# A graph and feed-forward kernel: one of nine one-hot columns moves from VectorE to ScalarE in the last adding stage

## The reference, cut to what matters

```
time_feat = relu(edge_attr @ W_time.T + b_time)          # (212500, 64)
sums      = segment_sum(time_feat, src, n)               # (12500, 64)
counts    = segment_sum(ones, src, n)
node_time = sums / max(counts, 1)
fused     = relu([relu(ln(x) @ W_down.T + b_down), node_time] @ W_fusion.T + b_fusion)
x = x + ln(x) + fused @ W_up.T + b_up
x = x + shared_mlp(ln(x)) + top2_of_4_experts(ln(x))
```

## Time and profile before

| | us |
|---|---|
| median of 3 runs | 2168.73 |
| lowest and highest | 2162.14, 2173.69 |
| profiled execution | 2177.41 |
| its span | 2175.5 |

### The profile page before, as it was taken

The page is one execution under the profiler, slowest core; times in us unless marked ns, Lnnn a source line. Parts: engine busy times, 40 slices in busy tenths (PEclk is TensorE's granted clock), DMA queues, the critical chain, the costliest instruction groups (busy, mean ns, idle before and its releaser), DMA issues.

```text
span 2175.5 us, 75498 instructions
## 1 busy us (share of the span) xinstructions
PE 2000.5 (92%) x26922; PEld 1672.3 (77%) x26946; DVE 1779.5 (82%) x5883; ACT 1404.0 (65%) x3239; POOL 1069.4 (49%) x918
## 2 busy tenths in 40 slices
PE   4788888999999999999999999677869999999998
PEld 1576776799988899999899999677756667666666
DVE  9788999899988999998788887688966767767675
ACT  2598898999989888888988887000014444444443
POOL 0577777778787777787777776100011111111110
PEclk7699999999999999999999999899989999999999
DMA  2244343677766677776778776676731111212110
GB/s 85 71 127 122 126 126 122 189 213 208 211 198 180 205 219 220 217 217 200 208 226 245 239 223 183 178 205 184 205 96 44 53 58 44 66 44 66 44 54 31
DMA packets 239411, 323.68 MB, mean 149 GB/s; under 512 B 42144, under 2 KB 213965, under 8 KB 238706
## 3 DMA queue, kind: packets, MB, share of 16 engines
q1 hardware_dynamic: 176564, 192.90, 32.6%
q0 software_dynamic: 41504, 103.41, 13.0%
q10 hardware_dynamic: 20970, 22.54, 3.7%
HBM read 186.34 MB, written 175.77 MB: 166 GB/s over the span
## 4 chain that ended last, share of the span: by engine, by line
PE 71%; DVE 11%; DMA 5%; ACT 5%; issue 4%; SPq 1%; DVEq 1%; ACTq 1%; POOL 1%; POOLq 0%
PE moved L686 16%; PE bank L715 15%; PE bank L803 10%; PE bank L672 7%; PE moved L816 7%; PE bank L690 4%; DMA arena<-table 3%; DVE arena L1133 2%; PE bank L843 2%; DMA table<-arena 2%; DVE arena L1134 2%; PE bank L699 2%; ACT arena L1590 1%; DVE arena L1334 1%; ACT arena L1596 1%
## 5 line engine op out<-in xcount | busy, mean ns | idle before, releaser
L1812 POOL DMA_INDIRECT table<-arena x832 | 970.3, 1166 | 377.2 <-issue 262.3
L1596 ACT ACTIVATE arena<-moved 128x588 bf16<-128x588 f32 x832 | 547.0, 662 | 108.2 <-PE moved L686 91.7
L686 PE MATMUL moved<-arena 128*128 128x196 bf16 x4992 | 590.5, 254 | 7.8 <-ACT arena L1596 6.7
L686 PEld LDWEIGHTS moved<-arena 128*128 128x128 f16 x4992 | 453.6, 98 | 79.8 <-ACT arena L1596 19.1
L1590 ACT ACTIVATE arena<-bank 128x512 f32<-128x512 f32 x624 | 371.0, 595 | 84.0 <-PE bank L672 68.0
L1235 DVE TENSOR_TENSOR sums<-sums,bank 128x130 f32 x816 | 232.0, 284 | 109.4 <-PE bank L715 88.9
L715 PE MATMUL bank<-arena 128*128 128x64 bf16 (+1 forms) x7344 | 273.4, 194 | 37.2 <-DVE sums L1235 24.6
L715 PE MATMUL bank<-arena,w_all 128*128 128x64 bf16 (+1 forms) x7344 | 272.4, 194 | 19.4 <-DVE sums L1235 18.9
L1711 ACT ACTIVATE arena<-bank,w_all 128x512 f32<-128x512 f32 (+1 forms) x225 | 152.8, 679 | 207.8 <-PE bank L803 116.6
L715 PEld LDWEIGHTS bank<-arena 128*128 128x128 bf16 x7344 | 254.7, 98 | 41.7 <-DVE arena L1215 41.7
L715 PEld LDWEIGHTS bank<-arena,w_all 128*128 128x128 bf16 x7344 | 254.2, 98 | 23.8 <-DVE w_all L1215 23.7
(11 more groups left out here) (292 smaller groups left out, 2864.8 us busy)
## 6 DMA issues: line engine op xcount, KB each, us to landing
arena<-table SPq DMA_DIRECT2D x672, 147.0 KB
arena<-in_attr SPq DMA_DIRECT2D x208, 144.0 KB
arena<-table ACTq DMA_DIRECT2D x144, 147.0 KB
table<-arena POOLq DMA_INDIRECT x832
x_ln<-arena SPq DMA_DIRECT2D x98, 128.0 KB
arena<-in_x SPq DMA_DIRECT2D x97, 128.0 KB
arena<-x_ln SPq DMA_DIRECT2D x24, 512.0 KB, 4.6
out_rows<-arena SPq DMA_DIRECT2D x24, 512.0 KB, 3.2
```

The source lines that it names most:

```text
L686: mm = e.matmul(moved8[:, 4 * (n % 2) + h, 0:PW], slot_hot[s % NSLOT][:, t, h * P:(h + 1) * P], upper(s, 0, PW)[:, t, :], start=j == 0, st ...
L1596: e.activation(row_buf[n % NROWS], moved8[:, 4 * (n % 2):4 * (n % 2) + 3, 0:PW], ACT.Copy).then_inc(s_rows, 1)
L1812: e.indirect_dma_start(out=table, out_offset=bass.IndirectOffsetOnAxis(ap=dest[s % NDEST][:, a:a + 1], axis=0), in_=row_buf[n % NROWS].rea ...
```

## The change

For loads 2 to 95 of the last part, VectorE's comparison of the third third covers two columns and not three. The ninth column is made by ScalarE: Square of (number - iota), with the column of numbers as bias, into a scratch `apart`, then Relu of (1 - that), which is one where the two are equal and zero elsewhere. `apart` lies in the first scatter buffer. In ScalarE's program the passes for load n+1 stand behind its DMA issues of iteration n. TensorE waits for the new semaphore `s_hot_last` before the third third of such a load.

```diff
+        apart = row_buf[0].rearrange("p h w -> p (h w)")[:, 0:NODES_A_BUCKET]
...
+        def last_by_scalar(k, n, c):
+            return k == LAST and n >= 2 and c == CL - 1
...
             def add_up(k, n, c):
                 t = sum_first[k] + n
                 e.wait_ge(s_hot, CL * t + c + 1)
+                if last_by_scalar(k, n, c):
+                    e.wait_ge(s_hot_last, n - 1)
...
             def hot_piece(k, n, c):
                 t = sum_first[k] + n
-                lo_of = tab[t % NTB].rearrange("p c r (h w) -> p (c r h) w", h=BLOCK)[:, c * PIECE:(c + 1) * PIECE, LO:LO + 2]
-                e.tensor_tensor(in_pairs(hot[t % 2][:, c * PIECE:(c + 1) * PIECE]), pairs(iota_lo, PIECE), each_pair(lo_of, NODES_A_BUCKET), ALU.is_equal).then_inc(s_hot, 1)
+                columns = slice(c * PIECE, (c + 1) * PIECE - last_by_scalar(k, n, c))
+                lo_of = tab[t % NTB].rearrange("p c r (h w) -> p (c r h) w", h=BLOCK)[:, columns, LO:LO + 2]
+                e.tensor_tensor(in_pairs(hot[t % 2][:, columns]), pairs(iota_lo, columns.stop - columns.start), each_pair(lo_of, NODES_A_BUCKET), ALU.is_equal).then_inc(s_hot, 1)
...
+            def last_column(n):
+                t = sum_first[LAST] + n
+                e.wait_ge(s_table[t % NTB], 16 * CL * (t // NTB + 1))
+                at = (CL * BLOCK - 1) * PW + LO
+                lo_of = tab[t % NTB].rearrange("p c r w -> p (c r w)")[:, at:at + 1]
+                if n > 2:
+                    e.wait_ge(s_hot_last, n - 2)
+                e.activation(apart, iota_lo, ACT.Square, bias=lo_of, scale=-1.0).then_inc(s_apart, 1)
+                e.wait_ge(s_apart, n - 1)
+                e.wait_ge(s_sum_ps, CL * (t - 1))
+                e.activation(hot[t % 2][:, TC - 1], apart, ACT.Relu, bias=1.0, scale=-1.0).then_inc(s_hot_last, 1)
+
             for k, n in last_turns:
                 for m in turn_loads(k, n):
                     if m % 2:
                         load_chunks(e, row_reg, k, m, m == 1)
+                if 2 <= n + 1 < loads[k]:
+                    last_column(n + 1)
```

More of the change, by code:

```diff
@@ L121, in gnn_ffn @@
         s_unused = sem("s_unused")
-        s_hot, s_sum_ps, s_added = sem("s_hot"), sem("s_sum_ps"), sem("s_added")
+        s_hot, s_apart, s_hot_last, s_sum_ps, s_added = sem("s_hot"), sem("s_apart"), sem("s_hot_last"), sem("s_sum_ps"), sem("s_added")
         s_mean_a, s_square_a, s_sd_a, s_rs_a = sem("s_mean_a"), sem("s_square_a"), sem("s_sd_a"), sem("s_rs_a")
```

## The result

| | before | after |
|---|---|---|
| median us (12 runs each) | 2169.45 | 2178.63 |
| lowest, highest | 2162.14, 2174.45 | 2174.28, 2183.86 |
| ratio | | 1.0045, 95% interval 1.0033 to 1.0057 |

The change makes the kernel 9 us slower, between 7 and 12. The forecast was 2.9 us slower; the time lies inside the range and just short of the 0.5% bound. (That bound was set too wide: twelve runs a side tell 0.12% here.) The sign was right and the size was a third of the truth, so the working has to be gone through term by term.

A forecast was written before the change was run, and what follows sets the result against it. The adding stretch was taken as bound by the time from a free buffer to a landed load; -2.4 was eaten by ScalarE's lateness, +2.2 net, plus +0.7 gave +2.9 us on 2168.7: 2171.6, range 2160 to 2183.

The forecast's parts named there:

- 0.5% bound: Whole kernel: the prediction held that a measurement can't tell less than about 0.5% (10.8 us) from no change.
- What bounds the stretch: Adding of table loads, 1370 to 1599 us: bound by free buffer to landed load, 19 hops of 9.5 us.
- (1): VectorE's third comparison, 768 to 512 elements: 0.13 us less a turn, in 18 turns only, -2.4 us.
- the 18 turns between hops: Adding stretch: of 94 steps, 76 lie in 19 four-load buffer-to-landing hops; the other 18 run at VectorE's pace.
- (2): ScalarE's new passes per load: Square 0.51 us, Relu 0.46, each hand-over 0.05; bounds per pass 0.42 and 0.60.
- (3): Odd loads' third piece about 0.5 us late behind ScalarE's issues and passes; 9 odd free turns, +2.2 us.
- Rival C: ScalarE sets the pace: a pair of loads takes 4.9 us, about 22 pairs grow; +12 us, 2181; chance 0.15.
- (4): Odd loads' issues wait for the even column before: 7 hops at 0.1 us each, +0.7 us.
- (5): TensorE's 94 more waits between pieces of a load: 0.
- B: ScalarE's work is free, issues run ahead; only the 18 turns shrink, -2.4 us, 2166.3; chance 0.25.
- D: Hops shorten too as loads land earlier; VectorE's saving arrives whole, -12.2 us, 2156; chance 0.05.
- 1.2 us a dip: Side risk: after a 2.56 us wait TensorE ran a load in 2.99 us, not 1.82; 1.2 us a case.

The follow-up runs named there:

- Five buffers: The kernel before with a fifth buffer for the last part's table loads, iteration n issuing load n+4: ratio 0.9929, -15 us.
- cut_only: The change without ScalarE's passes and TensorE's wait for them; VectorE compares eight columns, nobody makes the ninth: ratio 1.0017 against the kernel before, +4 us.
- cut_first: As cut_only, but the shortened comparison is the turn's first, not its third: ratio 1.0015 against the kernel before, +3 us.
- scatter run: The kernel before, unchanged, submitted as if it were a change: ratio 1.0009, +2 us.
- passes_waited: As passes_only, but TensorE waits for ScalarE before the third piece, as in the change: ratio 1.0053 against the kernel before, +11.5 us.
- passes_only: The change with VectorE making all nine columns, ScalarE's Relu writing to an unread scratch, TensorE not waiting: ratio 1.0018 against the kernel before, +4 us.
- the split issues: The kernel before, with SyncE issuing the first two chunks of every last-part load and ScalarE the third: ratio 0.9959, -9 us.
- the change on top of five buffers: The change with a fifth buffer and each load's issues split between SyncE (two chunks) and ScalarE (one): ratio 0.9909 against the kernel before, -20 us.

## Why the prediction was right in sign and small in size

**What bounds the stretch**: right. VectorE at 2.0 us a turn is the pace only when nothing is late, and the time from a free buffer to a landed load is what makes 2.3 of it. Five buffers show it.

**(1) VectorE, -2.4 us**: the price was right (an undisturbed turn of 1.87 us), the gain is not seen. cut_only and cut_first are both some 1 to 2 us above the scatter run, not below it. The saving went into waits, for landings above all. That the 18 turns between hops would keep their share assumed that no other load is about to become the late one; that this is the reason was not tested.

**(2) Prices of the passes**: right, 0.508 and 0.418 us. An odd column is ready 3.6 us after TensorE's release in the median (3.5 worked out), and TensorE resumes 0.10 us later (0.14).

**(3) TensorE's wait in odd loads**: the failed term. The wait itself was right, 0.58 us a time against 0.5, in odd loads only, behind issue, Square and Relu. But I let it count in 9 odd loads, those of the 18 free turns, and held that a landing wait in the same pair would hide it. It shows in 28 of 47 (I had said under half), and 10 of the 28 stand in a pair in which VectorE waited over 0.5 us for a landing. A pause within an odd load moves TensorE's end, and with it the release of the load four later, so it can lengthen a hop. The wait is worth 8 to 9 us (passes_waited less passes_only) where I had +2.2 us net of VectorE's saving, some 4.5 without it. Rival C had counted 22 pairs without a landing wait; the same 0.5 us in those, and nothing saved, would have given 11.

**And its tail**: I took the issue at 0.34 us, the median of the earlier trace rows, beside a maximum of 1.5. Long issues add up to 11.8 us in the trace after, and they stand right before passes that TensorE waits for. How much of the loss is theirs was not measured; passes_waited, with 7.2 us of them, loses as much.

**(4) Late odd issues, +0.7 us**: small, as said. passes_only, where they are late, is 0 to 8 us slower, of which 2 may be scatter; in the change's own trace they are not late.

**(5) More waits on TensorE for nothing**: right; even loads run their 54 matmuls in one piece.

**Rivals.** B (free work) is out, and so is D. C, the slower one, had more of it than the forecast. The page after gives ScalarE 147 us of idle time before its Squares, but that is no spare time, since a sequencer's DMA issues are not counted as busy: the 2.80 us before the Square at 1445.82 above are filled by three issues (1443.05 + 2.67). With the issues counted, ScalarE is unoccupied for only some 10 of the 224 us from its first Square to its last Relu, and the chain of the stretch runs for rounds on end from issue to passes to the next issue. So ScalarE was full, as C said. But full alone costs little: passes_only has the same passes, is unoccupied for 8 of 214 us, and is 2 to 4 us slower. What costs is that TensorE waits for a column which stands behind the issues.

**What was luck.** The measured 0.45% lies between the forecast's 0.13% and C's 0.55%. That it lies inside the range is owed to C's end of it, and that it is still "no change" by the 0.5% bound is a matter of 1 us. The forecast's own +2.9 us is outside the measured 7 to 12.

**The clock.** The first profile of the kernel before and that of after have two dips each to 1.2 GHz within the stretch (granted clock 0.5, 3.4 us each, behind the low clock of its first 11 us, which all three have), the second profile of the kernel before has none of them; at the 1.2 us a dip of the prediction that is some 2 us between single profiles. It does not explain the loss: the granted clock of the change's twelve runs is 0.973 in the median, that of 29 runs of the kernel before 0.972.

## What to carry to other kernels

Spare time on an engine is not spare if it also issues DMAs. The earlier trace rows has ScalarE busy for 0.0 us in this stretch, yet its 48 rounds of three issues took 121 us of it. What counts is where in its program the new work stands, what the issue before it takes at its worst, and who waits for the result. Never put a wait for a landing before the issue of a later load on the same engine unless the chain spans as many loads as there are buffers. And before work is moved off the busiest engine, ask whether its waits would only grow: here the fifth buffer gave 15 us and the moved work at best 4.

## What was not expected of the hardware

A DMA issue takes 0.34 us in most cases and now and then 1.0 to 1.8 us, on SyncE (up to 1.1 us in the trace after) and ScalarE. What holds it up was not found.

When TensorE is nearly always busy in this stretch it pauses within a load, between matmuls where the program has no wait: 12 pauses over 0.06 us, 5.9 us in all, with five buffers, 16 and 7.9 us with the split issues, 4 and 2.9 us in the change as given, one or none in the two profiles of the kernel before. The view puts them down to "issue", as here with five buffers:

```profile
1441.07 0.23 PE L731 MATMUL bank<-arena,w_all 128*128 128x64 bf16 x2 [0.88 <-issue]
```

Their places are the same in every kernel. If the stretch's 5184 matmuls are counted through, all such pauses of all traces lie 124 or 125 matmuls apart, or a multiple of that (this one stands before matmul 1726, counted from 0; others stand before 1601, 1975 and 2099). The page has a queue for instructions:

```profile
q8 instruction: 218, 3.57, 0.7%
```

That is 16.4 KB a transfer, and 41 of them start in the stretch, one for about 125 matmuls. Of the 95 such pauses in all traces 90 end 1.1 to 1.6 us after one of these transfers has landed, whatever the pause's own length, the other five within 2.4 us (here the transfer landed at 1439.52 us, and the pause ended at 1441.07). So these are, by all that the traces show, waits of TensorE for its own next instructions; why they come late at some places and in time at others no run shows. They may be a part of why neither the split issues nor the change on top of five buffers gave what VectorE's and ScalarE's rows promised.
